# One-hot comparisons of a token sort on bfloat16 operands with the token tile as innermost index

## The chip, the cores and the metric

The kernel runs on one core of one Trainium2 chip. The metric is the device time of one execution in microseconds. Each kernel was executed several times; the median is what counts.

## The reference, cut to what matters

```python
x = L0_attn_x                      # (16, 256, 128) float32
xn = _layernorm(x)
s = attention(xn, ...)             # 16 heads of 8, LoRA weights, alibi slopes, causal, softmax
# routed feed-forward: each of the 4096 tokens belongs to one of 8 experts
indices = argmax(softmax(xn @ Wr + br))
for i in range(8):
    xi = xn * (indices == i)
    h = relu(xi @ W1[i] + b1[i])   # (128 -> 512)
    out += h @ W2[i] + b2[i]       # (512 -> 128)
return x + s * silu(out)
```

## The kernel before

The 4096 tokens are 32 tiles (`NT`) of 128 tokens; token tiles are sequences cut in two. The attention is a loop over `NB` = 16 sequences `i`, each with six groups `g` of score units; every engine's program is this same loop, and other work is hung into it by places `(i, g)` written out by hand at the top of the file. TensorE computes at the same time the scores of sequence i and the row maxima's scores of sequence i + 2. VectorE reduces those maxima (`unit_max`, L812). Four PSUM banks rotate for VectorE's results and three for ScalarE's, so TensorE waits for the reader of a bank's last use.

Beside this, the tokens are sorted by expert. `choose()` on VectorE (L925 to L929, place (1, 0)) makes the expert one-hot; `keep_logits` (L908, L913) comes just ahead of it. TensorE counts and ranks it (`count_tiles` L1213, `rank` L1220 and L1224), and VectorE works out for each token its slot: a tile of 128 rows (`SLOT_ROWS` = 40 of them) and a row in it (`token_slots`, L956 to L963). Then the inverse of this map is made with one-hot matrices:

- `tile_onehot` (VectorE, place (1, 4), L969 and L971) compares each token's slot tile with 0, 128, 256, ...; the second output is that one-hot times the token's place in its token tile.
- `tile_numbers` (GpSimd, place (1, 4), L546) multiplies the first in place by the token tile's number. `fill_v` (L540) and `max_parts` (L573 to L581) stand behind it in GpSimd's queue.
- `row_onehot(c)` (VectorE, L977, places (1, 5), (2, 0), (2, 1), (2, 2)) compares each token's row with 0 to 127, for eight token tiles at a time.
- `slot_tokens` (TensorE, place (2, 3), L1235) multiplies the two with 32 products, one for each token tile, which gives for each slot the token in it.
- `keep_ids` (VectorE, L983 to L988) turns that into `from_row` and `token_of`. GpSimd's `fetch_rows` (L532) gathers the rows by indirect DMA from (2, 4) on, TensorE turns them (`turn_rows`, L1351, first at (3, 2)) and the 39 expert tiles follow (`hidden` L1359, `output` L1367), one every few groups, almost to the end of the loop.

In the same places TensorE also projects sequence i + 4 (`project`, L1183), whose remainder VectorE takes (`remainder`, L856), ScalarE rounds (`second_part`, L658) and GpSimd splits once more (`third_part`, L519); and it makes the experts' constant rows at (2, 1) and (2, 2) (L1381, L1390). L511, L565 and L589 are GpSimd's memset and copies at the start, L522 its normalisation.

In the kernel before, the slot values are float32 (`r32`), the constants they are compared with are float32 for the tiles (`iota_slot`) and bfloat16 for the rows (`iota_row`), and the outputs are laid out with the token tile outside and the compared index innermost.

Of the kernel before, what the change touches and what calls it, by code (L numbers as in the profile page):

```python
# [25 lines left out]
BF16 = mybir.dt.bfloat16  # L26
I32 = mybir.dt.int32
U32 = mybir.dt.uint32
ALU = mybir.AluOpType
# [3 lines left out]
P = 128  # L33
NB, T, D = 16, 256, 128
NT = NB * T // P
# [6 lines left out]
E, HID = 8, 512  # L42
# [5 lines left out]
SLOT_ROWS = (SLOT_TILES + 3) // 4 * 4  # L48
# [4 lines left out]
ROUND = float(3 * P << 22)  # L53
# [64 lines left out]
CHOOSE_AT, COUNT_AT, RANK_AT, SLOTS_AT = (1, 0), (1, 1), (1, 2), (1, 3)  # L118
TILE_HOT_AT = (1, 4)
ROW_HOT_AT = {(1, 5): 0, (2, 0): 1, (2, 1): 2, (2, 2): 3}  # L120
IDS_AT, TILE_EXPERTS_AT = (2, 3), (2, 4)
PROJECT_FIRST = {6: 2, 8: 3}
TURN_FIRST = {(0, 4): 2, (0, 7): 3, (0, 9): 4}
# [86 lines left out]
def program(nc, x, w_dense, lora, br, b1, w_experts, const_f32, const_bf16, const_rows, zero_rows, out):  # L210
# [14 lines left out]
    with ctx:  # L225
        def sb(name, shape, dt=F32):
            return ctx.enter_context(nc.sbuf_tensor(name, shape, dt))

        def sem(name):
# [13 lines left out]
        iota_slot = cf[:, 2 * P + 8:2 * P + 8 + SLOT_ROWS]  # L243
        place1 = cf[:, 2 * P + 52:2 * P + 53]
        tile_ids = cf[:, 2 * P + 64:2 * P + 64 + NT]
# [9 lines left out]
        iota_row = cb[:, 2 * BLK + 2 * P + 2 * (NT + 1) * E + 2:]  # L255
# [7 lines left out]
        hT = sb("hT", [P, 2, NC_H, P])  # L263
# [25 lines left out]
        onehot_b = sb("onehot_b", [P, NT, E], BF16)  # L289
        tile_counts = sb("tile_counts", [P, 2, P], BF16)  # L290
        r32 = sb("r32", [P, 6, NT])
        r32i = sb("r32i", [P, 2, NT], I32)
        r40 = sb("r40", [P, 2, SLOT_ROWS])
        r8 = sb("r8", [P, 8, E])
        r8i = sb("r8i", [P, 2, E], I32)
        te_cmp = sb("te_cmp", [1, SLOT_TILES, E])
        te_f = sb("te_f", [1, 2, SLOT_TILES])
        tile_expert = sb("tile_expert", [1, SLOT_TILES], I32)
# [25 lines left out]
        xsT_slot = sb("xsT_slot", [P, 2, 4, P])  # L324
        crow_sb = sb("crow_sb", [P, D])
        w_flat = w_slots[:, :, :].rearrange("p r f -> p (r f)")
        row_hot = w_flat[:, 0:NT * P // 2].bitcast(BF16).rearrange("p (n m) -> p n m", m=P)
        tile_hot = w_flat[:, NT * P // 2:NT * P // 2 + NT * SLOT_ROWS].bitcast(BF16).rearrange("p (n c h) -> p n c h", c=2, h=SLOT_ROWS)
        rt = xs_slot[:, :, :, :].rearrange("p r j d -> p (r j d)")[:, 0:3 * NT * E].rearrange("p (c n) -> p c n", c=3)
        y_slot = sb("y_slot", [P, 3, D])  # L330
        y_tok = xn_all
# [3 lines left out]
        names = """x_in0 x_in1 x_in2 x_in3 x_in4 dense_in ident_in constants_in masks_in later_in br_in b1_in b1_pad b1_spread nmax_r2 zero_src lora_ps w_eff_done experts_in  # L335
            var_done std_done nmr_done dve_seq xn_vec xn_pool xn_act logits_turned_done part1_done part2_done part3_done
            q1_out0 q1_out1 q1_out2 q1_out3 q2_out0 q2_out1 q2_out2 q2_out3 q3_out0 q3_out1 q3_out2 q3_out3 nmax_zero max_zeroed0 max_zeroed1
            const_rows0 const_rows1 const_rows2 vd_zero vd_one onehot_done slots_done tile_place_done tile_hot_done row_hot_done rows_done tokens_done rows_kept tile_expert_done
            max_in0 max_in1 nmax1 nmax_r nmax2 nmax3
            v_done x_again0 x_again1 x_again2 x_again3 pv_ps pv_read rz_done o_norm_done oT_done b1_done b1_cols_done crow_diag_done  # L340
            w_done xs_in0 xs_in1 xs_in2 xs_in3 xs_in4 xs_in5 xs_in6 xs_in7 y_out0 y_out1 y_out2
# [2 lines left out]
        S = {n: sem(n) for n in names}  # L344
# [162 lines left out]
        def _(pool):  # L507
# [27 lines left out]
            def fill_v(b):  # L535
# [4 lines left out]
                pool.tensor_tensor(v_halves[b % 2][:, :, :, 0:DH], v_kept[:, b, :].rearrange("p (c d) -> p c d", d=DH).unsqueeze(2).to_broadcast(shape),  # L540
                                   of_half.unsqueeze(1).unsqueeze(3).to_broadcast(shape), ALU.mult).then_inc(S["v_done"], 1)

            def tile_numbers():

                pool.wait_ge(S["tile_place_done"], 1)
                pool.tensor_tensor(tile_hot[:, :, 1, :], tile_hot[:, :, 1, :], tile_ids.unsqueeze(2).to_broadcast([P, NT, SLOT_ROWS]),  # L546
                                   ALU.mult).then_inc(S["tile_hot_done"], 1)

            def scatter_y(t):
# [17 lines left out]
            def max_parts(b):  # L567

                r = b % 2
                for u in range(NU):  # L570
                    wait_vec_emptied(pool, "max", b, u)
                wait_act_full(pool, "nmax", b - 2)
                pool.tensor_scalar(nmax[r][:, :, 0, :], row_max[r][:, :, :], -1.0, None, ALU.mult).then_inc(S["nmax1"], 1)  # L573
                pool.wait_ge(S["nmax1"], b + 1)
                pool.tensor_tensor(nmax_rem[:, :, :], row_max[r][:, :, :], nmax[r][:, :, 0, :], ALU.add).then_inc(S["nmax_r"], 1)
                pool.wait_ge(S["nmax_r"], b + 1)
                pool.tensor_scalar(nmax[r][:, :, 1, :], nmax_rem[:, :, :], -1.0, None, ALU.mult).then_inc(S["nmax2"], 1)
                pool.wait_ge(S["nmax2"], b + 1)
                pool.tensor_tensor(nmax_rem2[:, :, :], nmax_rem[:, :, :], nmax[r][:, :, 1, :], ALU.add).then_inc(S["nmax_r2"], 1)
                pool.wait_ge(S["nmax_r2"], b - 1)  # L580
                pool.tensor_scalar(nmax[r][:, :, 2, :], nmax_rem2[:, :, :], -1.0, None, ALU.mult).then_inc(S["nmax3"], 1)  # L581
# [23 lines left out]
            for i in range(NB):  # L605
                for g, units in enumerate(GROUPS):
                    for t in FETCH_AT.get((i, g), ()):
                        wait_act_full(pool, "scores", i, units[0])
                        fetch_rows(t)
                    if g == PROJECT + 2 and i + AHEAD < NB:  # L610
                        third_part(i + AHEAD)
                    for t in range(SLOT_TILES):
                        if SCATTER_TURNS[t] == i * NG + g:
                            if g in (0, 3):
                                wait_act_full(pool, "scores", i, units[1])
                            elif TILES_AT[i, g][0] < SLOT_TILES:
                                wait_vec_full(pool, "hidden", TILES_AT[i, g][0])
                            scatter_y(t)
                    if g == 0 and 0 < i < NB - 1:
                        max_parts(i + 1)  # L620
                    if (i, g) == TILE_HOT_AT:
                        tile_numbers()
                    if i + 1 < NB and g == FILL_V:
                        fill_v(i + 1)
# [167 lines left out]
        def _(dve):  # L792
            seq = [0]

            def then(ins):

                seq[0] += 1
                ins.then_inc(S["dve_seq"], 1)
                dve.wait_ge(S["dve_seq"], seq[0])
# [65 lines left out]
            for n in range(2):  # L865
                last = dve.scalar_tensor_tensor(w_eff[:, n, :], pv_bank[:, n * P:(n + 1) * P], LORA_SCALE, w_raw[:, n, :], ALU.mult, ALU.add)
# [85 lines left out]
            def token_slots():  # L952

                maxima_between(*SLOTS_AT, 0)
                bank, emptied = wait_vec_full(dve, "rank")
                dve.tensor_tensor(m3[1], bank[:, 0:NT * E].rearrange("p (n e) -> p n e", e=E),  # L956
                                  r8[:, 4, :].unsqueeze(1).to_broadcast(shape), ALU.add).then_inc(emptied, 1)
                wait_vec_emptied(dve, "rank")
                then(dve.tensor_tensor(m3[2], m3[1], onehot_b[:, :, :], ALU.mult))
                chained(dve.tensor_reduce(r32[:, 3, :], m3[2], AX.X, ALU.add), SLOTS_AT, 1)  # L960
                then(dve.tensor_scalar(r32[:, 2, :], r32[:, 3, :], -(P - 1) / 2, ROUND, ALU.add, ALU.add))
                dve.scalar_tensor_tensor(r32[:, 5, :], r32[:, 2, :], ROUND, r32[:, 3, :], ALU.subtract, ALU.subtract)
                dve.tensor_scalar(r32[:, 4, :], r32[:, 2, :], ROUND, None, ALU.subtract).then_inc(S["slots_done"], 1)  # L963
                dve.wait_ge(S["slots_done"], 1)

            def tile_onehot():

                hot = [P, NT, SLOT_ROWS]
                then(dve.tensor_tensor(tile_hot[:, :, 1, :], iota_slot.unsqueeze(1).to_broadcast(hot),  # L969
                                       r32[:, 4, :].unsqueeze(2).to_broadcast(hot), ALU.is_equal))  # L970
                dve.tensor_scalar(tile_hot[:, :, 0, :], tile_hot[:, :, 1, :], place1, None, ALU.mult).then_inc(S["tile_place_done"], 1)  # L971

            def row_onehot(c):

                dve.wait_ge(S["later_in"], 16)
                hot = [P, 8, P]
                dve.tensor_tensor(row_hot[:, 8 * c:8 * (c + 1), :], iota_row.unsqueeze(1).to_broadcast(hot),  # L977
                                  r32[:, 5, 8 * c:8 * (c + 1)].unsqueeze(2).to_broadcast(hot), ALU.is_equal).then_inc(S["row_hot_done"], 1)

            def keep_ids():  # L980

# [17 lines left out]
            for b in range(2):  # L999
                for u in range(NU):  # L1000
                    if b == 0 or not STATISTICS_FIRST <= u < STATISTICS_FIRST + 3:
                        unit_max(b, u)
                    for n in MOMENTS_FIRST.get((b, u), ()):
                        last = moments(1 + n // 8, n, n + 1)
# [66 lines left out]
            for i in range(NB):  # L1071
                for g, units in enumerate(GROUPS):
# [44 lines left out]
                    if (i, g) in GATED_AT:  # L1117
                        c = GATED_AT[i, g]
# [11 lines left out]
            bank, _ = wait_act_full(dve, "s", NB - 1)  # L1130
# [6 lines left out]
        def _(pe):  # L1137
# [89 lines left out]
            def slot_tokens():  # L1227


                pe.wait_ge(S["tile_hot_done"], 1)  # L1230
                bank, full = begin_vec("ids")
                for n in range(NT):
                    if n % 8 == 0:
                        pe.wait_ge(S["row_hot_done"], n // 8 + 1)
                    last = pe.matmul(bank[:, 0:2 * SLOT_ROWS], row_hot[:, n, :], tile_hot[:, n].rearrange("p c h -> p (c h)"),  # L1235
                                     start=(n == 0), stop=(n == NT - 1))
                last.then_inc(full, 1)

# [315 lines left out]
```

## Time and profile before

| | |
|---|---|
| median of 3 runs | 296.31 us (295.81 to 296.85) |
| profiled execution | 296.07 us |
| its span, first to last instruction | 294.2 us |
| mean granted TensorE clock | 0.983 |
| TensorE busy | 267.8 us, 91% |
| VectorE busy | 228.1 us, 78% |
| ScalarE busy | 185.5 us, 63% |
| GpSimd busy | 152.6 us, 52% |

The span is shorter than the time, as the time also holds the start and the end of the program. Times of instructions are measured from the span's start. PE is TensorE, DVE VectorE, ACT ScalarE, POOL GpSimd.

### The profile page before, as it was taken

The page shows a single profiled execution, that of the slowest core. Times are in us where ns is not written, and L with a number is a line of the kernel's source. Part 1 is how long each engine was busy: PE and PEld are TensorE (multiplying, and loading weights), DVE is VectorE, ACT ScalarE, POOL GpSimd, SP SyncE. Part 2 cuts the span into 40 slices and gives each one's busy share as a digit, 9 for nine tenths or more (in the row PEclk, how much of TensorE's full clock was granted, in tenths as well). Part 3 has the DMA queues.
Part 4 walks back from the last instruction along what each step waited for, and adds up shares of the span by engine and source line. Part 5 has one row for each costly group of instructions (what it writes and reads, how often), then busy time and mean ns, then how long its engine had stood idle before and what let it go on. Part 6 is the DMA issues. An engine that isn't in the chain of part 4 may idle for free.

```text
span 294.2 us, 12787 instructions
## 1 busy us (share of the span) xinstructions
PE 267.8 (91%) x5196; PEld 203.6 (69%) x5196; DVE 228.1 (78%) x483; ACT 185.5 (63%) x331; POOL 152.6 (52%) x226
## 2 busy tenths in 40 slices
PE   7899999684996999999999999999999999979962
PEld 3556555353674788888887888888788888856641
DVE  3788999789987578596868768685875868676996
ACT  3335355444466668777777778777776876558960
POOL 3073293115436577866677667667766533343100
PEclk9999999979999799999999999999999999999997
DMA  4799556687415442332425433231524623108553
GB/s 137 207 240 212 127 166 194 203 240 225 112 36 134 109 126 67 95 97 57 108 55 129 123 101 84 74 91 51 133 51 96 147 54 90 30 29 250 138 163 111
DMA packets 50970, 35.98 MB, mean 122 GB/s; under 512 B 5112, under 2 KB 48376, under 8 KB 50784
## 3 DMA queue, kind: packets, MB, share of 16 engines
q1 hardware_dynamic: 46680, 28.89, 37.0%
q0 software_dynamic: 2496, 5.12, 7.0%
q10 hardware_dynamic: 1736, 1.15, 1.6%
q8 instruction: 42, 0.69, 1.0%
q14 instruction: 16, 0.13, 0.2%
HBM read 15.28 MB, written 6.75 MB: 75 GB/s over the span
## 4 chain that ended last, share of the span: by engine, by line
PE 68%; DVE 18%; issue 6%; DMA 3%; POOL 2%; SPq 1%; ACT 1%; ACTq 0%; DVEq 0%; POOLq 0%
PE bank L1359 14%; PE bank L1367 12%; PE bank L1273 11%; PE bank L1324 10%; PE bank L1183 4%; DVE row_max L812 4%; PE bank L1281 3%; PE bank L1343 3%; PE bank L1253 2%; PE bank L1190 2%; DVE xn_all L1063 2%; PE bank L1351 2%; DVE w_slots L977 2%; DVE xn_all L1057 1%; DVE o_turned L1020 1%
## 5 line engine op out<-in xcount | busy, mean ns | idle before, releaser
L812 DVE TENSOR_REDUCE row_max<-bank 128x2 f32<-128x512 f32 (+3 forms) x176 | 105.6, 627 | 19.2 <-PE bank L1261 16.3
L757 ACT ACTIVATE probs<-bank 128x512 f32<-128x512 f32 (+1 forms) x176 | 89.5, 558 | 46.4 <-PE bank L1281 46.1
L1273 PE MATMUL bank<-qk_stack 64*64 64x64 bf16 (+3 forms) x1024 | 60.8, 237 | 6.5 <-ACT probs L757 3.3
L1253 PE MATMUL bank<-qk_stack 64*64 64x64 bf16 (+3 forms) x1024 | 61.7, 237 | 1.1 <-DMA qk_stack<-parts 0.7
L554 POOL DMA_INDIRECT expert_rows<-y_slot,token_of x39 | 38.6, 990 | 37.2 <-PE bank L1359 22.8
L532 POOL DMA_INDIRECT xs_slot<-normalised_rows,from_row x39 | 39.7, 1018 | 24.9 <-PE bank L1281 17.9
L1273 PEld LDWEIGHTS bank<-qk_stack 64*64 64x64 bf16 x1024 | 34.3, 108 | 23.6 <-issue 10.7
L739 ACT ACTIVATE w_slots<-w_all 128x1156 f32 x39 | 45.5, 1167 | 4.0 <-issue 3.4
L1324 PE MATMUL bank<-probs,v_diag 128*32 128x64 f32 (+3 forms) x1024 | 46.5, 311 | 1.2 <-issue 1.0
L1045 DVE TENSOR_TENSOR hT<-bank,w_slots 128x512 f32<-128x512 f32 x39 | 27.0, 691 | 23.3 <-PE bank L1359 23.3
L1359 PE MATMUL bank<-xsT_slot,w_slots 128*128 128x128 f32 x312 | 44.6, 286 | 0.2 <-issue 0.2
L1281 PE MATMUL bank<-cb 64*64 64x128 bf16 (+2 forms) x352 | 43.7, 243 | 0.0
L1261 PE MATMUL bank<-cb 64*64 64x128 bf16 (+2 forms) x352 | 43.3, 243 | 0.0
L1367 PE MATMUL bank<-w_slots,hT 128*128 128x128 f32 x312 | 41.3, 276 | 0.0
L1359 PEld LDWEIGHTS bank<-xsT_slot,w_slots 128*128 128x128 f32 x312 | 38.0, 192 | 2.8 <-issue 0.8
L1367 PEld LDWEIGHTS bank<-w_slots,hT 128*128 128x128 f32 x312 | 38.0, 192 | 0.1
L1253 PEld LDWEIGHTS bank<-qk_stack 64*64 64x64 bf16 x1024 | 33.7, 108 | 5.6 <-issue 4.2
L1324 PEld LDWEIGHTS bank<-probs,v_diag 128*32 128x32 f32 x1024 | 25.2, 111 | 12.5 <-issue 2.3
L519 POOL TENSOR_TENSOR parts<-rem,parts 128x512 bf16<-128x512 f32 x15 | 17.5, 1165 | 18.0 <-ACT parts L658 17.7
L1183 PE MATMUL bank<-xnT_all,w_eff 128*128 128x256 f32 x64 | 17.8, 403 | 3.5 <-DVE row_max L812 2.7
L540 POOL TENSOR_TENSOR v_diag<-x_all,cf 128x512 f32<-128x512 f32 x16 | 17.9, 1118 | 6.0 <-ACT x_all L662 5.7
L1281 PEld LDWEIGHTS bank<-cb 64*64 64x64 bf16 x352 | 20.0, 109 | 0.0
(132 smaller groups left out, 346.1 us busy)
## 6 DMA issues: line engine op xcount, KB each, us to landing
qk_stack<-parts SPq DMA_DIRECT2D x120, 64.0 KB, 2.1
qk_stack<-parts SPq DMA_DIRECT2D x32, 128.0 KB, 2.8
w_all<-w_experts SPq DMA_DIRECT2D x8, 512.0 KB, 4.6
x_all<-x SPq DMA_DIRECT2D x7, 512.0 KB, 5.2
normalised_rows<-xn_all SPq DMA_DIRECT2D x4, 512.0 KB, 5.2
xn_all<-expert_rows SPq DMA_DIRECT2D x8, 256.0 KB, 5.2
out<-xn_all SPq DMA_DIRECT2D x7, 256.0 KB, 3.2
xs_slot<-normalised_rows,from_row POOLq DMA_INDIRECT x39, 3.2
```

Source lines behind the costliest of these rows:

```text
L532: pool.indirect_dma_start(xs_slot[:, q % 2, t % 4, :], None, xn_dram[:, :], bass.IndirectOffsetOnAxis(from_row[:, t:t + 1], axis=0)).then_ ...
L554: pool.indirect_dma_start(y_dram[:, :], bass.IndirectOffsetOnAxis(token_of[:, t:t + 1], axis=0), y_slot[:, t % 3, :], None).then_inc(S[f"y ...
L739: act.activation(w_slot[t % 3], w_all[:, bass.ds(e, 1), :].rearrange("p o f -> p (o f)"), ACT.Copy).then_inc(S["w_done"], 1)
L757: act.activation(probs[:, m % PROBS, 0:w], bank[:, 0:w], ACT.Exp).then_inc(emptied, 1)
L812: dve.tensor_reduce(row_max[b % 2][:, n, pairs[0]:pairs[-1] + 1], bank[:, 0:ln_u * len(pairs)].rearrange("p (c k) -> p c k", k=ln_u), AX.X ...
L1253: pe.matmul(bank[to, c * ln_u:(c + 1) * ln_u], q[rows, p, n * BLK:(n + 1) * BLK], k[rows, p, 0:(n + 1) * BLK], start=(c == 0), stop=False, ...
L1261: last = pe.matmul(bank[to, 0:ln_u * len(pairs)].rearrange("p (c k) -> p c k", k=ln_u)[:, :, n * BLK:], ident_b[rows, rows], mask_qk[rows] ...
L1273: pe.matmul(bank[rows, c * ln_u:(c + 1) * ln_u], k[rows, p, kb * BLK:(kb + 1) * BLK], q[rows, p, kb * BLK:], start=(c == 0), stop=False, s ...
L1281: last = pe.matmul(bank[rows, 0:ln_u * len(pairs)].rearrange("p (c k) -> p c k", k=ln_u)[:, :, 0:BLK], ident_b[rows, rows], mask_kq[rows]. ...
L1324: last = pe.matmul(pv_bank[32 * j:32 * j + 32, half * T + kb * BLK:(half + 1) * T], v_diag[b % 2][:, kb, p, :], probs[:, (b * NU + w) % PR ...
L1359: last = pe.matmul(bank[:, c * P:(c + 1) * P], w_slot[t % 3][:, c * P:(c + 1) * P], xsT_slot[:, t // 4 % 2, t % 4, :], start=(c == 0), sto ...
L1367: last = pe.matmul(bank[:, 0:D], hT[:, t % 2, c, :], w_slot[t % 3][:, W2 + c * D:W2 + (c + 1) * D], start=(c == 0), stop=(c == NC_H - 1))
```

## The change

The slot tile and the row of each token are written as bfloat16 into `place_slot`. Both one-hot arrays are laid out with the token tile innermost. The constants they are compared with, `iota_row` and `iota_slot`, are spread by GpSimd into full arrays, each number repeated 8 or 32 times, in bfloat16: 1024 and 1280 elements on each partition, at place (1, 1), in memory of `hT` and `xsT_slot` that isn't in use yet. VectorE then compares contiguous bfloat16 arrays with the slot values, repeated over the outer index. TensorE reads both operands of `slot_tokens` with a step: its weights every 8th element, its moving operand every 32nd. Two arrays that nothing uses are removed.

```diff
+IOTAS_AT = (1, 1)
...
-        r32i = sb("r32i", [P, 2, NT], I32)
+        place_slot = sb("place_slot", [P, 2, NT], BF16)
...
-        r8i = sb("r8i", [P, 2, E], I32)
...
-        row_hot = w_flat[:, 0:NT * P // 2].bitcast(BF16).rearrange("p (n m) -> p n m", m=P)
-        tile_hot = w_flat[:, NT * P // 2:NT * P // 2 + NT * SLOT_ROWS].bitcast(BF16).rearrange("p (n c h) -> p n c h", c=2, h=SLOT_ROWS)
+        row_hot = w_flat[:, 0:NT * P // 2].bitcast(BF16).rearrange("p (c m n) -> p c m n", m=P, n=8)
+        tile_hot = w_flat[:, NT * P // 2:NT * P // 2 + NT * SLOT_ROWS].bitcast(BF16).rearrange("p (c h n) -> p c h n", c=2, n=NT)
+        rows_iota = hT[:, 0].rearrange("p c k -> p (c k)").bitcast(BF16).rearrange("p (m n) -> p m n", n=8)
+        slots_iota = xsT_slot[:, :, :, :].rearrange("p r j k -> p (r j k)")[:, 0:SLOT_ROWS * NT // 2].bitcast(BF16).rearrange("p (h n) -> p h n", n=NT)
...
+            def spread_iotas():
+
+                pool.wait_ge(S["lora_ps"], 1)
+                pool.wait_ge(S["later_in"], 16)
+                pool.tensor_copy(rows_iota, iota_row.unsqueeze(2).to_broadcast([P, P, 8])).then_inc(S["iotas_done"], 1)
+                pool.tensor_copy(slots_iota, iota_slot.unsqueeze(2).to_broadcast([P, SLOT_ROWS, NT])).then_inc(S["iotas_done"], 1)
+
             def tile_numbers():
 
                 pool.wait_ge(S["tile_place_done"], 1)
-                pool.tensor_tensor(tile_hot[:, :, 1, :], tile_hot[:, :, 1, :], tile_ids.unsqueeze(2).to_broadcast([P, NT, SLOT_ROWS]),
+                pool.tensor_tensor(tile_hot[:, 1], tile_hot[:, 1], tile_ids.unsqueeze(1).to_broadcast([P, SLOT_ROWS, NT]),
                                    ALU.mult).then_inc(S["tile_hot_done"], 1)
...
-                dve.scalar_tensor_tensor(r32[:, 5, :], r32[:, 2, :], ROUND, r32[:, 3, :], ALU.subtract, ALU.subtract)
-                dve.tensor_scalar(r32[:, 4, :], r32[:, 2, :], ROUND, None, ALU.subtract).then_inc(S["slots_done"], 1)
+                dve.scalar_tensor_tensor(place_slot[:, 0, :], r32[:, 2, :], ROUND, r32[:, 3, :], ALU.subtract, ALU.subtract)
+                dve.tensor_scalar(place_slot[:, 1, :], r32[:, 2, :], ROUND, None, ALU.subtract).then_inc(S["slots_done"], 1)
...
-                hot = [P, NT, SLOT_ROWS]
-                then(dve.tensor_tensor(tile_hot[:, :, 1, :], iota_slot.unsqueeze(1).to_broadcast(hot),
-                                       r32[:, 4, :].unsqueeze(2).to_broadcast(hot), ALU.is_equal))
-                dve.tensor_scalar(tile_hot[:, :, 0, :], tile_hot[:, :, 1, :], place1, None, ALU.mult).then_inc(S["tile_place_done"], 1)
+                hot = [P, SLOT_ROWS, NT]
+                dve.wait_ge(S["iotas_done"], 2)
+                then(dve.tensor_tensor(tile_hot[:, 1], slots_iota, place_slot[:, 1, :].unsqueeze(1).to_broadcast(hot), ALU.is_equal))
+                dve.tensor_scalar(tile_hot[:, 0], tile_hot[:, 1], place1, None, ALU.mult).then_inc(S["tile_place_done"], 1)
...
-                dve.wait_ge(S["later_in"], 16)
-                hot = [P, 8, P]
-                dve.tensor_tensor(row_hot[:, 8 * c:8 * (c + 1), :], iota_row.unsqueeze(1).to_broadcast(hot),
-                                  r32[:, 5, 8 * c:8 * (c + 1)].unsqueeze(2).to_broadcast(hot), ALU.is_equal).then_inc(S["row_hot_done"], 1)
+                hot = [P, P, 8]
+                dve.tensor_tensor(row_hot[:, c], rows_iota, place_slot[:, 0, 8 * c:8 * (c + 1)].unsqueeze(1).to_broadcast(hot),
+                                  ALU.is_equal).then_inc(S["row_hot_done"], 1)
...
+                    if (i, g) == IOTAS_AT:
+                        spread_iotas()
...
-                    last = pe.matmul(bank[:, 0:2 * SLOT_ROWS], row_hot[:, n, :], tile_hot[:, n].rearrange("p c h -> p (c h)"),
+                    last = pe.matmul(bank[:, 0:2 * SLOT_ROWS].rearrange("p (c h) -> p c h", c=2), row_hot[:, n // 8, :, n % 8], tile_hot[:, :, :, n],
```

## Rows read from the trace of the kernel before

**Rows 1.** The profile's page, busy time of each engine in us, its share and instructions.
```profile
PE 267.8 (91%) x5196; PEld 203.6 (69%) x5196; DVE 228.1 (78%) x483; ACT 185.5 (63%) x331; POOL 152.6 (52%) x226
```

**Rows 2.** Stretch, length, busy us of PE, PEld, DVE, ACT, POOL; clock; DMA share.
```profile
60.00:61.50 1.50, 1.50 (x24) 0.77 (x16) 1.50 (x5) 0.86 (x2) 0.01 (x1) 0.50 0.91 180
...
70.80:73.40 2.60, 0.00 (x0) 0.00 (x0) 2.60 (x3) 0.83 (x2) 2.60 (x2) 1.00 0.46 108
...
83.80:95.70 11.90, 9.46 (x257) 6.49 (x257) 10.16 (x24) 8.10 (x16) 7.61 (x12) 1.00 0.36 92
...
97.00:260.00 163.00, 162.66 (x3180) 135.91 (x3183) 117.36 (x227) 117.68 (x192) 104.43 (x135) 0.99 0.34 87
```

**Rows 3.** Timeline of VectorE, 67 to 84 us: start, duration, instruction, idle time before it.
```profile
67.20 1.48 DVE L969 TENSOR_TENSOR w_slots<-cf,r 128x1280 bf16<-128x1280 f32 x1
68.72 0.55 DVE L971 TENSOR_SCALAR w_slots<-w_slots,cf 128x1280 bf16<-128x1280 bf16 x1
...
69.79 2.98 DVE L977 TENSOR_TENSOR w_slots<-cb,r 128x1024 bf16<-128x1024 bf16 x1
...
73.89 1.21 DVE L977 TENSOR_TENSOR w_slots<-cb,r 128x1024 bf16<-128x1024 bf16 x1
...
78.49 0.68 DVE L856 TENSOR_TENSOR rem<-bank,parts 128x512 f32<-128x512 f32 x1
...
80.36 1.86 DVE L977 TENSOR_TENSOR w_slots<-cb,r 128x1024 bf16<-128x1024 bf16 x1
...
83.86 0.20 DVE L983 COPY r<-bank 128x40 f32<-128x40 f32 x1 [0.65 <-PE bank L1235]
```

**Rows 4.** Timeline of TensorE, 73 to 95 us.
```profile
73.43 1.13 PE L1183 MATMUL bank<-xnT_all,w_eff 128*128 128x256 f32 x4 [2.71 <-DVE row_max L812]
...
79.32 2.02 PE L1390 MATMUL bank<-crow_sb,cf 128*128 128x128 f32 x16 [0.64 <-DVE rem L856]
...
82.50 1.32 PE L1235 MATMUL bank<-w_slots 128*128 128x80 bf16 x32
...
94.65 0.33 PE L1351 MATMUL bank<-cf,xs_slot 128*128 128x128 f32 x1 [1.73 <-DMA xs_slot<-normalised_rows,from_row]
```

**Rows 5.** Timeline of GpSimd, 53 to 86 us.
```profile
53.17 0.29 POOL L581 TENSOR_SCALAR nmax<-nmax_rem 128x32 bf16<-128x32 f32 x1
61.49 1.16 POOL L519 TENSOR_TENSOR parts<-rem,parts 128x512 bf16<-128x512 f32 x1 [8.04 <-ACT parts L658]
69.36 2.34 POOL L546 TENSOR_TENSOR w_slots<-w_slots,cf 128x1280 bf16<-128x1280 bf16 x1 [6.71 <-DVE w_slots L971]
...
79.99 1.16 POOL L519 TENSOR_TENSOR parts<-rem,parts 128x512 bf16<-128x512 f32 x1 [3.70 <-ACT parts L658]
85.37 1.18 POOL L532 DMA_INDIRECT xs_slot<-normalised_rows,from_row  x1 [4.23 <-issue]
```

**Rows 6.** Timelines of VectorE and TensorE around `choose()`.
```profile
55.24 0.22 DVE L913 TENSOR_TENSOR logits<-logits_turned,br_sb 128x64 f32<-128x64 f32 x1
...
55.95 0.42 DVE L926 TENSOR_TENSOR xs_slot<-logits,r 128x256 f32<-128x256 f32 x1
...
57.80 0.20 PE L1213 MATMUL bank<-cb,onehot_b 128*128 128x1 bf16 x2 [1.37 <-DVE onehot_b L929]
```

**Rows 7.** Timelines of VectorE and of GpSimd near 25 us.
```profile
25.13 0.93 DVE L913 TENSOR_TENSOR logits<-logits_turned,br_sb 128x64 f32<-128x64 f32 x1
...
24.83 1.15 POOL L519 TENSOR_TENSOR parts<-rem,parts 128x512 bf16<-128x512 f32 x1 [3.09 <-ACT parts L658]
```

**Rows 8.** Instructions of three lines on GpSimd, ns least/median/most.
```profile
L565 POOL COPY b_cols<-b_sb x4: 197/198/198, 31.0 to 31.4; 128x8 f32<-128x8 f32 x4
...
L589 POOL COPY v_diag<-cf x2: 288/288/289, 11.8 to 12.0; 128x64 f32<-128x64 f32 x2
...
L511 POOL MEMSET v_diag<- x2: 951/953/955, 0.9 to 1.8; 128x1024 f32 x2
```

**Rows 9.** The chain that ended last, in order of time: start, us, what.
```profile
106.44 1.09 PE bank L1359 x8
```

More of the change, by code:

```diff
@@ L337, in program @@
             q1_out0 q1_out1 q1_out2 q1_out3 q2_out0 q2_out1 q2_out2 q2_out3 q3_out0 q3_out1 q3_out2 q3_out3 nmax_zero max_zeroed0 max_zeroed1
-            const_rows0 const_rows1 const_rows2 vd_zero vd_one onehot_done slots_done tile_place_done tile_hot_done row_hot_done rows_done tokens_done rows_kept tile_expert_done
+            const_rows0 const_rows1 const_rows2 vd_zero vd_one onehot_done iotas_done slots_done tile_place_done tile_hot_done row_hot_done rows_done tokens_done rows_kept tile_expert_done
             max_in0 max_in1 nmax1 nmax_r nmax2 nmax3
```

## The prediction

> **What bounds the kernel now.** I read the busy shares first [rows 1]: TensorE is busy for 91% of the span, VectorE for 78%. That is an average, so I then read the stretches [rows 2]. From 97 to 260 us TensorE is busy for 162.66 of 163.00 us: nothing the diff touches runs there, and whatever moves the start of that stretch moves the end by as much. The edit sits ahead of it. From 70.80 to 73.40 us TensorE does nothing at all while VectorE is busy for all of it, and from 83.80 to 95.70 TensorE works 9.46 of 11.90 us.
>
> Next, the timeline of VectorE [rows 3]. From 67.20 until it waits for the products at 83.86 the listing marks no idle time, and both comparisons are in it: the tile comparison (1.48 us), its scaling (0.55), and four row comparisons of 1.21 us. Two of the four show more, 2.98 and 1.86. Beside them GpSimd runs L546 from 69.36 to 71.70 and L519 from 79.99 to 81.15 [rows 5]; 71.70 + 1.07 is 72.77, and 81.15 + 1.07 is 82.22, just where the two comparisons end. So a VectorE comparison with two SBUF inputs that starts while GpSimd reads SBUF waits for the whole GpSimd instruction.
>
> TensorE's timeline [rows 4] shows who waits for VectorE: projection L1183 at 73.43 after 2.71 us idle (its bank comes free from a maximum that stands behind the first row comparison), and L1390 at 79.32 after 0.64 us, released by L856, which stands behind the third. From 79.32 TensorE has no gap until the 32 products of `slot_tokens` at 82.50. These release L983 at 83.86, which leads to `from_row`; GpSimd starts its first fetch at 85.37 [rows 5], and fetches 0 to 3 with other work run one behind another until TensorE turns the rows at 94.65, after 1.73 us idle on that DMA. The chain that sets the end therefore goes: VectorE to 79.2, TensorE to 83.8, VectorE, GpSimd and DMA to 94.65, TensorE from there.
>
> **Removed: element time on VectorE.** L969 (1280 elements, 1.48 us) and L977 (1024, 1.21) give a line of 1.05 ns an element plus 0.14. After the change all operands are bfloat16 and innermost contiguous. The trace has no such two-input operation. Bounds: no gain, 1.21; or the rate of L971, 1280 bfloat16 elements with one input in 0.55, which is 0.32 ns an element and gives 0.47. Between them I take half the element time, as this one reads two streams where L971 reads one: 0.68 for a row comparison and 0.81 for the tile comparison, so 0.53 less for each of four and 0.67 less. The Trainium skill (VectorE: DVE Perf Modes, the perf-mode tier table) has `tensor_tensor` on bfloat16 in SBUF at twice the rate and never at four times, which is the value I take; no row here shows it. L971 itself, now on contiguous data, I leave at 0.55 (at most 0.07 to gain).
>
> What of this lies on the path: L969 ends 0.67 earlier, so L971, then GpSimd's L546, start 0.67 earlier (L546 keeps its 2.34). The first row comparison still waits for it and ends 0.67 + 0.53 = 1.20 earlier, at 71.57. L1183 goes with it, to 72.2. The second and third comparison add 1.07, so L856 ends 2.27 earlier, near 76.9. TensorE cannot follow all of that: after L1183, its work up to L1390 takes the same 5.25 us less the small wait of 0.06 for a maximum within it (none is then left), so L1390 comes at 77.3 to 77.4, 2.0 us earlier, now bound by TensorE. The fourth comparison is worth nothing: GpSimd's L519 comes after ScalarE's copy of L856's result, near 77.7 to 78.9, the comparison waits for it again and ends near 79.4, and `slot_tokens` comes at 80.5; what hides it is TensorE's own work from L1390 on, and without that cover 0.53 more would count. The fetches behind it are ordered by GpSimd and by TensorE's own scores, which shift alike. **Minus 2.0 us.**
>
> **Added: two copies on GpSimd.** `spread_iotas` stands at (1, 1), behind `max_parts(2)`, whose last instruction ends at 53.46 [rows 5]. Its semaphores are long set, so it starts near 53.5. GpSimd's next work is L519 at 61.49, so its own queue has room. The cost lies elsewhere: `choose()` runs on VectorE at that time, on the path, since TensorE waits 1.37 us for L929 before it can count [rows 6]. L913, L926, L927 and L929 have two SBUF inputs; L908, L925 and L928 have one or read PSUM. What that means is seen at 25.13: the same L913 takes 0.93 us instead of 0.22 and ends at 26.06, as L519 on GpSimd ends at 25.98 [rows 7]. The Trainium skill (SBUF — State Buffer, Who interferes with whom) says the same: a two-input VectorE instruction and a GpSimd one that reads SBUF exclude each other for the whole instruction. By that rule, too, nothing before 57.7 is safe unless the copies are done; the trace agrees.
>
> How long the copies take: GpSimd's COPY takes 198 ns for 8 elements and 288 for 64 [rows 8], which is 1.6 ns an element: 1.8 us for 1024, 2.2 us for 1280. The lower bound is a memset of 1024 in 0.95, which reads nothing: 0.95 and 1.2. At the COPY rate the first ends about 55.3, L913 (due at 55.24) slips in between, the second runs 55.5 to 57.7, and L926, due at 55.95, ends near 57.9 instead of 56.37: 1.5 us. If the second copy gets in ahead of L913, it is 57.5 against 55.46: 2.1 us. At the memset rate the second ends at 55.7 and L913 is held 0.4 us. I take **plus 1.5 us**, between 0.4 and 2.1, as the COPY rows are the same operation. It is passed on in full: VectorE, and TensorE behind L929, have no slack of that size before 66 us.
>
> **Changed: TensorE's operands in `slot_tokens`.** Weights now step 8 elements (16 bytes) and the moving operand 32 elements (64 bytes). Today 32 products with contiguous operands take 1.32 us, 41 ns each [rows 4]. No row has a strided operand. Bounds: nothing, and 136 ns each, the rate of a float32 product (8 in 1.09 us [rows 9]), which is 4.4 us, plus 3.0. The nearest row is the same product with contiguous data, so I stay near it, at half a doubling: **plus 0.65 us**. All of it is on the path. The Trainium skill (SBUF — State Buffer, Door 1: The DMA port swizzle) speaks against the change: it gives 16-byte cache lines and a penalty when each access goes to another line, as here in both operands. It names no factor; this is the third rival.
>
> **Sum.** -2.0 + 1.5 + 0.65 = +0.15 us on the profiled execution's 296.07 us (span 294.2 and 1.9 around it). The median of the runs shown is 296.31, so 0.24 above it; the sum gives 296.2 to 296.5 and I say 296.4. Removing `r32i` and `r8i` and the bfloat16 outputs of L962 and L963 (32 elements, fixed cost) change nothing. What a measurement can tell from no change is 0.3%, 0.9 us.
>
> **Cases.**
> 1. The saving is eaten by the copies and the strides: copies 1.5, strides 0 to 1.3. 295.5 to 297.3, likeliest 296.4; 0.42.
> 2. Faster: the copies run near the memset's rate and are over by 55.7. Then 0.4 replaces 1.5, and with unslowed products -2.0 + 0.4 = -1.6, 294.7. For it: every other GpSimd row has a second input, pointer scalars or scattered output, while these copies write in order. It decides from the point where the sum of copies and strides is under 1.1 us. 0.28.
> 3. The products slow down by a doubling or more. A doubling alone is 1.3 for 0.65, +0.8, 297.1; the float32 rate is 3.0, -2.0 + 1.5 + 3.0 = +2.5, 298.8. The row against it: weights of 128 columns load within 41 ns today, so there is spare rate. Slower from a total of 2.9 on: 0.14.
> 4. The second copy gets ahead of L913 (2.1) with a full doubling (1.3): +1.4, 297.7. TensorE's idle time before counting then also grows; its clock was granted at 0.50 (the 1.2 GHz level) from 60.00 to 61.50 [rows 2] after it had been mostly idle, so this may grow. 0.09.
> 5. The edit doesn't do what it says: the comparisons stay at one element a pass, the saving is nothing, +1.5 + 0.65 = +2.15, 298.5. For it: no two-input row is faster than 1.05 ns. Against: L971 shows that the engine does go faster on bfloat16. 0.07.
>
> Faster 0.28, same 0.42, slower 0.30. The range of 8 in 10, 294.6 to 298.2, takes in case 2 and leaves out the far parts of 3 and 5; the likeliest case's own is 295.5 to 297.3.
>
> **What the next profile would show.** Row comparisons of 0.68 us where GpSimd is quiet and the first ending with L546 (wrong: 1.21, or 0.47). Two COPY rows on GpSimd of 1.8 and 2.2 us from 53.5, and L913 or L926 lengthened by the wait, with `onehot_b` done near 59.2 instead of 57.7. L1390 no longer waiting for L856. The 32 products in 1.3 to 2.6 us. `slot_tokens` ending near 84. The prediction is wrong if VectorE isn't held during `choose()`, if the 32 products take over 4 us, or if TensorE at 97 us and later starts at a time not shifted by the sum of these.

## The result and the profile after

The changed kernel takes 298.69 us, median of 17 runs, against 296.31 us for the kernel before in as many: ratio 1.0077, 95% interval 1.0053 to 1.0101, so 1.6 to 3.0 us slower. This is outside the range of the prediction (294.6 to 298.2) and on the side to which it gave 0.30. The execution profiled took 297.37 us, the lowest of the 17, with a span of 295.5.

Most of the difference stands in the line of the 32 products of `slot_tokens`, in TensorE's timeline of the changed kernel (start, duration). Its lines are numbered anew: L1245 is what was L1235, L1193 was L1183, L1400 was L1390, L1361 was L1351, and L1334 was L1324, the products of the probabilities with the values.

```profile
72.71 1.13 PE L1193 MATMUL bank<-xnT_all,w_eff 128*128 128x256 f32 x4 [1.19 <-DVE row_max L823]
...
77.66 2.05 PE L1400 MATMUL bank<-crow_sb,cf 128*128 128x128 f32 x16
...
80.87 4.71 PE L1245 MATMUL bank<-w_slots 128*128 128x80 bf16 x32
...
86.73 1.51 PE L1334 MATMUL bank<-probs,v_diag 128*32 128x192 f32 x16
...
97.24 0.33 PE L1361 MATMUL bank<-cf,xs_slot 128*128 128x128 f32 x1 [1.45 <-DMA xs_slot<-normalised_rows,from_row]
```

Beside [rows 4]: the projection comes 0.72 us earlier, L1400 no longer waits and comes 1.66 us earlier, the products start 1.63 us earlier, at 80.87 for 82.50. Then they take 4.71 us instead of 1.32, 147 ns each instead of 41. What was 1.63 us early is 1.76 late. Behind them come the products with the values, L1334, which take 1.51 us (the same work took 0.86 before), in a stretch in which TensorE's clock was granted below its full 2.4 GHz level for part of the time: 0.72 of it on the mean from 84 to 88 us, where the kernel before had 1.00. This is the listing by stretch:

```profile
84.00:88.00 4.00, 4.00 (x68) 2.79 (x66) 2.28 (x9) 1.20 (x2) 0.88 (x1) 0.72 0.01 4
```

The last turn of fetched rows (L1361) comes at 97.24 for 94.65, 2.59 us late. So 0.83 us more are lost behind the products. The fetches show where: GpSimd's first starts 1.75 us late (87.12 for 85.37), its second 2.42 (90.22 for 87.80), with the low clock between them. In `after_again` below, where the clock stayed full there, the first and the second are both 2.8 us late.

VectorE's timeline shows the comparisons (L981 was L969, L987 was L977) and the hold ahead of `choose()` (L919 was L908, L924 was L913, L940 was L929). By a hold I mean that an instruction is lengthened because GpSimd reads memory at the same time:

```profile
53.95 0.45 DVE L919 STREAM_TRANSPOSE logits_turned<-bank 128x256 f32<-128x256 f32 x1 [0.84 <-PE bank L1212]
54.44 1.15 DVE L924 TENSOR_TENSOR logits<-logits_turned,br_sb 128x64 f32<-128x64 f32 x1
...
57.44 0.42 DVE L940 TENSOR_TENSOR onehot_b<-cf,r 128x256 bf16<-128x256 f32 x1
...
67.39 0.81 DVE L981 TENSOR_TENSOR w_slots<-xsT_slot,place_slot 128x1280 bf16<-128x1280 bf16 x1
...
69.31 2.75 DVE L987 TENSOR_TENSOR w_slots<-hT,place_slot 128x1024 bf16<-128x1024 bf16 x1
...
73.18 0.68 DVE L987 TENSOR_TENSOR w_slots<-hT,place_slot 128x1024 bf16<-128x1024 bf16 x1
...
78.57 1.33 DVE L987 TENSOR_TENSOR w_slots<-hT,place_slot 128x1024 bf16<-128x1024 bf16 x1
...
85.61 0.20 DVE L993 COPY r<-bank 128x40 f32<-128x40 f32 x1 [4.04 <-PE bank L1245]
```

Against [rows 3] the comparisons have the durations that were forecast, 0.81 and 0.68 us. The first still waits for GpSimd (2.75 us), and so does the last (1.33). The idle time in the last line is new: VectorE, which had been the engine in front, now sits idle for 4.04 us until the products are done. This is GpSimd's timeline (L549 and L550 are the two copies, L555 was L546, L534 was L532):

```profile
53.27 1.03 POOL L549 COPY hT<-cb 128x1024 bf16<-128x1024 bf16 x1
54.26 1.25 POOL L550 CAST xsT_slot<-cf 128x1280 bf16<-128x1280 f32 x1
...
68.87 2.63 POOL L555 TENSOR_TENSOR w_slots<-w_slots,cf 128x1280 bf16<-128x1280 bf16 x1 [6.10 <-DVE w_slots L982]
...
87.12 1.18 POOL L534 DMA_INDIRECT xs_slot<-normalised_rows,from_row  x1 [7.77 <-PE bank L1291]
```

The copies end at 55.51, and L924, due at 54.44, takes 1.15 us instead of 0.22 and ends at 55.59, 0.93 us late. L555 takes 0.29 us more than before [rows 5] in the new layout.

### The profile page after: what moved, and what is told of

Its sections match the earlier page's. It is cut to its first block, busy times and chain, and to the rows that moved or that the text cites. A ratio compares the mean times of both kernels' runs of the same rounds, so it can differ in the third digit from the quotient of the medians.

```text
span 295.5 us, 12790 instructions
## 1 busy us (share of the span) xinstructions
PE 272.2 (92%) x5196; PEld 207.3 (70%) x5196; DVE 226.6 (77%) x483; ACT 185.5 (63%) x331; POOL 154.2 (52%) x228
## 3 DMA queue, kind: packets, MB, share of 16 engines
q10 hardware_dynamic: 1736, 1.15, 1.6%
## 4 chain that ended last, share of the span: by engine, by line
PE 72%; DVE 16%; issue 4%; DMA 3%; POOL 1%; SPq 1%; ACT 1%; ACTq 0%; DVEq 0%; POOLq 0%
PE bank L1369 14%; PE bank L1377 12%; PE bank L1283 11%; PE bank L1334 11%; PE bank L1193 4%; DVE row_max L823 3%; PE bank L1291 3%; PE bank L1353 3%; PE bank L1263 2%; PE bank L1200 2%; DVE xn_all L1073 2%; PE bank L1361 2%; PE bank L1245 2%; DVE xn_all L1067 1%; PE bank L1167 1%
## 5 line engine op out<-in xcount | busy, mean ns | idle before, releaser
L534 POOL DMA_INDIRECT xs_slot<-normalised_rows,from_row x39 | 39.7, 1018 | 27.6 <-PE bank L1291 24.8
L1283 PEld LDWEIGHTS bank<-qk_stack 64*64 64x64 bf16 x1024 | 34.7, 109 | 23.8 <-issue 11.9
L1334 PE MATMUL bank<-probs,v_diag 128*32 128x64 f32 (+3 forms) x1024 | 46.8, 311 | 1.2 <-issue 1.0
L1369 PE MATMUL bank<-xsT_slot,w_slots 128*128 128x128 f32 x312 | 44.2, 285 | 0.2 <-issue 0.2
L1369 PEld LDWEIGHTS bank<-xsT_slot,w_slots 128*128 128x128 f32 x312 | 37.8, 191 | 2.8 <-issue 0.8
L1263 PEld LDWEIGHTS bank<-qk_stack 64*64 64x64 bf16 x1024 | 34.2, 108 | 5.5 <-issue 4.1
L1334 PEld LDWEIGHTS bank<-probs,v_diag 128*32 128x32 f32 x1024 | 25.1, 111 | 12.8 <-issue 2.6
L1291 PEld LDWEIGHTS bank<-cb 64*64 64x64 bf16 x352 | 20.1, 109 | 0.0
L1271 PEld LDWEIGHTS bank<-cb 64*64 64x64 bf16 x352 | 19.8, 109 | 0.0
```

The lines of the kernel that those rows point to most:

```text
L534: pool.indirect_dma_start(xs_slot[:, q % 2, t % 4, :], None, xn_dram[:, :], bass.IndirectOffsetOnAxis(from_row[:, t:t + 1], axis=0)).then_ ...
L1263: pe.matmul(bank[to, c * ln_u:(c + 1) * ln_u], q[rows, p, n * BLK:(n + 1) * BLK], k[rows, p, 0:(n + 1) * BLK], start=(c == 0), stop=False, ...
L1271: last = pe.matmul(bank[to, 0:ln_u * len(pairs)].rearrange("p (c k) -> p c k", k=ln_u)[:, :, n * BLK:], ident_b[rows, rows], mask_qk[rows] ...
L1283: pe.matmul(bank[rows, c * ln_u:(c + 1) * ln_u], k[rows, p, kb * BLK:(kb + 1) * BLK], q[rows, p, kb * BLK:], start=(c == 0), stop=False, s ...
L1291: last = pe.matmul(bank[rows, 0:ln_u * len(pairs)].rearrange("p (c k) -> p c k", k=ln_u)[:, :, 0:BLK], ident_b[rows, rows], mask_kq[rows]. ...
L1334: last = pe.matmul(pv_bank[32 * j:32 * j + 32, half * T + kb * BLK:(half + 1) * T], v_diag[b % 2][:, kb, p, :], probs[:, (b * NU + w) % PR ...
```

## The experiments

Twelve runs in three groups of four: nine other kernels, two of them measured twice, and the changed kernel once more. Each group was measured beside the kernel before on a chip of its own. The kernel before took 303.1 us in the first group, 296.1 in the second and 296.5 in the third, so ratios to it are compared, not times. Every listing has the line numbers of its own kernel. "Packed" below means that TensorE reads an operand's elements one next to the other.

**Which operand costs: `weights_packed` and `moving_packed`.**

```diff
-        row_hot = ....rearrange("p (c m n) -> p c m n", m=P, n=8)
+        row_hot = ....rearrange("p (n m) -> p n m", m=P)
...
-                dve.tensor_tensor(row_hot[:, c], rows_iota, place_slot[:, 0, 8 * c:8 * (c + 1)].unsqueeze(1).to_broadcast(hot),
+                dve.tensor_tensor(row_hot[:, 8 * c:8 * (c + 1), :], iota_row.unsqueeze(1).to_broadcast(hot),
+                                  place_slot[:, 0, 8 * c:8 * (c + 1)].unsqueeze(2).to_broadcast(hot), ...
```

> The changed kernel with the row one-hot back in its old layout (TensorE's weights contiguous) and its moving operand still stepping 64 bytes. Theory A, the moving operand's step is what costs: the 32 products stay near 4.7 us, and as the row comparisons are back at 1.21 us the kernel is some 3 to 4 us above the kernel before. Theory B, the weights' step is what costs: the products fall to some 1.3 us and the kernel is within 0.5 us of the kernel before. Theory C, both cost: 2 to 4 us.

`moving_packed` does the same to the tile one-hot and leaves the row one-hot as changed; its tile comparison then reads float32 constants again and takes 1.48 us.

> The changed kernel with the tile one-hot back in its old layout (moving operand contiguous) and the weights still stepping 16 bytes. Theory A (moving operand): products 1.3 us, kernel some 0.5 to 1 us below the kernel before, since the row comparisons stay at 0.68 us. Theory B (weights): products near 4.7 us, kernel 2 to 3 us above it. Theory C (both): 2 to 4 us of products.

`weights_packed`: ratio 1.0135 (1.0091 to 1.0178). `moving_packed`: 1.0017 (0.9982 to 1.0051). Their rows of the products in TensorE's timelines, first the one with contiguous weights:

```profile
82.19 4.54 PE L1245 MATMUL bank<-w_slots 128*128 128x80 bf16 x32
```

and then the one with a contiguous moving operand:

```profile
81.31 2.16 PE L1246 MATMUL bank<-w_slots 128*128 128x80 bf16 x32
```

So it is theory A for the size, with a part of C: the moving operand's step of 64 bytes alone makes 142 ns of each product, the weights' step of 16 bytes alone 68 ns, and both together are hardly more than the larger (147), not the sum. `moving_packed` was expected 0.5 to 1 us below the kernel before and is level with it within its interval: its weights cost 0.84 us and L924 is held for 0.93. In its profile the products end only 0.35 us before those of the kernel before (83.47 for 83.82).

`weights_packed` also has the row comparison on bfloat16 with one slot value repeated along the innermost index (a step of 0; ns least/median/most):

```profile
L987 DVE TENSOR_TENSOR w_slots<-cb,place_slot x4: 1209/1536/2498, 70.0 to 80.0; 128x1024 bf16<-128x1024 bf16 x4
```

Its least is 1209 ns, as with float32 slot values: the type alone buys nothing, the contiguous innermost index does.

**The copies alone: `copies_only`.** The kernel before with `spread_iotas` added and its semaphore waited for.

> The kernel before with the two GpSimd copies at (1, 1) and the wait for them added, and nothing else. If the hold of L913 is passed on in full, expert one-hot and all behind it come 0.9 us later and the kernel is 0.9 us above the kernel before. Rival: it is absorbed by TensorE's or the DMAs' waits up to 70 us, under 0.3 us.

Ratio 1.0013 (0.9985 to 1.0041). VectorE's timeline:

```profile
54.69 0.45 DVE L920 STREAM_TRANSPOSE logits_turned<-bank 128x256 f32<-128x256 f32 x1 [1.49 <-PE bank L1215]
55.18 0.49 DVE L925 TENSOR_TENSOR logits<-logits_turned,br_sb 128x64 f32<-128x64 f32 x1
```

The run doesn't tell the two readings apart by time (its interval holds 0 and 0.9 us), but the trace says why little is seen: here L925 came at 55.18, near the end of the copies, and was held 0.27 us. In the changed kernel's profile it came at 54.44 and was held 0.93. The 0.27 are passed on as far as the products, which start at 82.78 for 82.50.

**A layout between the two: `inner2`, `inner4`, `inner8`.** All comparisons stay contiguous in bfloat16, but only 2, 4 or 8 token tiles are innermost, in both one-hots. TensorE's steps become 4, 8 or 16 bytes, and the spread constants shrink with them (256 and 80 elements for two).

```diff
+IN = 2
...
+        row_hot = ....rearrange("p (c m n) -> p c m n", m=P, n=IN)
+        tile_hot = ....rearrange("p (c q h n) -> p c q h n", c=2, h=SLOT_ROWS, n=IN)
...
+                hot = [P, 8 // IN, P, IN]
+                dve.tensor_tensor(row_hot[:, 8 // IN * c:8 // IN * (c + 1)], rows_iota.unsqueeze(1).to_broadcast(hot),
+                                  place_slot[:, 0, 8 * c:8 * (c + 1)].rearrange("p (q n) -> p q n", n=IN).unsqueeze(2).to_broadcast(hot), ...
...
+                    ... row_hot[:, n // IN, :, n % IN], tile_hot[:, :, n // IN, :, n % IN], ...
```

> The changed kernel with only two token tiles innermost instead of 8 and 32: all operands of the comparisons still bfloat16 and contiguous innermost, TensorE's steps 4 bytes, the copied constants 256 and 80 elements. If the products pay for each access being on another 16-byte stretch, they fall back to 1.3 us; the copies end before L913's counterpart, so nothing is held in choose(); the comparisons keep 0.68 us, and the kernel is 1.5 to 2 us below the kernel before. Rival: any step but one element costs, products 3 us or more, kernel 1 us or more above it. Second rival: rows of two elements take the comparison back to 1.21 us, kernel as before.

> The kernel with two token tiles innermost once more, as a base for the three others: the interval of its ratio in the first run was 0.993 to 1.000. If the VectorE saving of some 2 us at the products is passed on, 0.993 to 0.997 of the kernel before; rival: given back by the granted clock, 0.999 to 1.002.

> Four token tiles innermost, both of TensorE's operands stepping 8 bytes, two of its elements in a 16-byte stretch. If what costs is an access in a new 16-byte stretch each time, the 32 products take 1.3 us as with a step of 4 bytes. Rival: the cost grows with the step, products between 1.4 and 2.4 us.

> Eight token tiles innermost in both, so the weights step 16 bytes as in the change and the moving operand 16 instead of 64. If the 16-byte stretch alone decides, the moving operand costs as much as at 64 bytes, 4.5 us for the products. Rival: the moving operand's cost depends on the size of its step, and at 16 bytes the products take what strided weights alone take, 2.2 us, or up to 3.

`inner2` gave 0.9963 (0.9926 to 1.0001) in the first group and 0.9946 (0.9911 to 0.9981) as `inner2_again`; `inner4` 0.9994 (0.9962 to 1.0026), `inner8` 1.0100 (1.0046 to 1.0155). The products of `inner2_again`, `inner4` and `inner8` in TensorE's timelines:

```profile
79.53 1.34 PE L1248 MATMUL bank<-w_slots 128*128 128x80 bf16 x32
```

```profile
81.22 2.60 PE L1248 MATMUL bank<-w_slots 128*128 128x80 bf16 x32
```

```profile
80.54 5.03 PE L1248 MATMUL bank<-w_slots 128*128 128x80 bf16 x32
```

This table has the 32 products by the step of the weights and of the moving operand, in bytes:

| weights | moving | kernel | us | ns each |
|---|---|---|---|---|
| 2 | 2 | before | 1.32 | 41 |
| 4 | 4 | inner2_again | 1.34 | 42 |
| 8 | 8 | inner4 | 2.60 | 81 |
| 16 | 16 | inner8 | 5.03 | 157 |
| 16 | 64 | after | 4.71 | 147 |
| 2 | 64 | weights_packed | 4.54 | 142 |
| 16 | 2 | moving_packed | 2.16 | 68 |

Where both operands step alike, 4 bytes are free, 8 double the product and 16 nearly double it again; taking the moving operand from 16 to 64 adds nothing. The clock is not the cause: it was granted in full during the products of the changed kernel, `after_again`, `strides_only` and `weights_packed`. Which operand makes the 81 ns at 8 bytes no run shows. For `inner4` my theory, that two elements in each 16-byte stretch are enough, was wrong, and its rival held in kind, though 2.60 us is above its 1.4 to 2.4. For `inner8` the theory held. The Trainium skill (SBUF — State Buffer, Door 1: The DMA port swizzle) has at least two accesses in a 16-byte line as enough to hide the memory's latency; here 8 bytes a step, two elements a line, costs 1.26 us over 32 products against 4 bytes, so the rows don't bear that part out, while they do bear out that 16 bytes and more are slow.

The comparison keeps its rate with rows of two elements, and with short copies L925 isn't held. The rows are those of `inner2`:

```profile
L989 DVE TENSOR_TENSOR w_slots<-hT,place_slot x4: 676/680/2448, 68.4 to 78.5; 128x1024 bf16<-128x1024 bf16 x4
L982 DVE TENSOR_TENSOR w_slots<-xsT_slot,place_slot x1: 815/815/815, 66.5 to 66.5; 128x1280 bf16<-128x1280 bf16 x1
...
54.67 0.23 DVE L925 TENSOR_TENSOR logits<-logits_turned,br_sb 128x64 f32<-128x64 f32 x1
```

**The products alone: `strides_only`.** The new layouts, but the comparisons read the constants unspread and there are no copies.

```diff
-                dve.tensor_tensor(row_hot[:, c], rows_iota, ...
+                dve.tensor_tensor(row_hot[:, c], iota_row.unsqueeze(2).to_broadcast(hot), ...
```

> The kernel before with nothing but the new layout of both one-hots: TensorE's operands step 16 and 64 bytes, while the comparisons read the constants unspread (innermost step 0) and no copies are made. If the products are what makes the change slower, they take 4.7 us here too, 3.4 us more on the path, and the kernel is 3 to 4 us above the kernel before (1.010 to 1.014), more than the changed kernel, which saves on VectorE. Rival: a part of the 3.4 us is absorbed by waits behind the products, under 1.006.

```profile
81.87 4.71 PE L1236 MATMUL bank<-w_slots 128*128 128x80 bf16 x32
```

**The changed kernel again, and with its copies on ScalarE: `after_again`, `copies_on_act`.**

> The changed kernel itself, as the control for the other runs of this call: 1.005 to 1.010 of the kernel before. Its profile also tells whether TensorE's clock falls right behind the slow products once more, as it did in the first profile (84 to 88 us at 0.72).

> The changed kernel with the two copies on ScalarE at (0, 5) instead of GpSimd at (1, 1). L913's counterpart takes 0.22 us again instead of 1.15. If that hold is passed on, the kernel is 0.9 us (0.3%) below the changed kernel of this call; rival: no difference, as the run with the copies alone had it (1.001 of the kernel before); second rival: slower, if ScalarE's 2 us of copies hold up its exponentials.

`strides_only` 1.0149 (1.0109 to 1.0189), `after_again` 1.0113 (1.0070 to 1.0157), `copies_on_act` 1.0074 (1.0045 to 1.0102). In `strides_only` the products take 4.71 us and the kernel is 3.2 to 5.6 us slower than before, a little above what was expected. That interval holds the 3.39 us of the products and excludes the rival, that a good part of them is absorbed behind them. Beside the products, GpSimd's product in place got slower by the layout (2.62 us for 2.34), and with it the row comparison that waits for it. `after_again` lies just above its expected 1.005 to 1.010, and the clock did not fall behind its products. `copies_on_act` is 0.4% below `after_again` by their ratios, but the intervals overlap, so that comparison is not decided. Its trace does show the hold gone:

```profile
54.62 0.23 DVE L925 TENSOR_TENSOR logits<-logits_turned,br_sb 128x64 f32<-128x64 f32 x1
```

and that of `after_again` shows it present, 0.88 us for the undisturbed 0.22:

```profile
55.73 0.88 DVE L924 TENSOR_TENSOR logits<-logits_turned,br_sb 128x64 f32<-128x64 f32 x1
```

**A version that beats both: `inner2_numbers`, and once more as `numbers_again`.** Two token tiles innermost, and the product with the tile number on VectorE, so that no GpSimd instruction stands in front of the first row comparison.

```diff
+                pool.tensor_copy(ids_b[:, :], tile_ids).then_inc(S["iotas_done"], 1)
...
+                dve.wait_ge(S["tile_place_done"], 1)
+                dve.tensor_tensor(tile_hot[:, 1], tile_hot[:, 1], ids_b[:, :].rearrange("p (q n) -> p q n", n=IN).unsqueeze(2).to_broadcast(hot), ALU.mult).then_inc(S["tile_hot_done"], 1)
...
-                        tile_numbers()
```

> Two token tiles innermost, and the product of the tile one-hot with the tile number moved from GpSimd to VectorE (bfloat16, 0.81 us), so that the first row comparison no longer waits for GpSimd. That comparison then takes 0.68 instead of 2.45 us, VectorE is 1 us further on, and if VectorE were the bound the kernel would be 1 us faster than with two innermost alone. Rival: the products come when TensorE has done its own work from the projection on, and the gain is what the projection comes earlier, 0.5 to 1 us; or nothing, if the clock or a DMA ends last.

> Two token tiles innermost and the tile numbers on VectorE once more, to settle whether it beats the kernel before and by how much: first interval 0.988 to 0.995, so 2 to 3 us below is expected; the rival is that a second call brings it to within 0.3%.

Ratios 0.9911 (0.9878 to 0.9945) and 0.9898 (0.9867 to 0.9930): 293.58 and 293.42 us, 1.6 to 3.6 and 2.1 to 3.9 us under the kernel before. These are VectorE's rows of `numbers_again`, by tile (ns least/median/most):

```profile
L985 DVE TENSOR_TENSOR w_slots<-hT,place_slot x4: 677/678/680, 69.8 to 77.3; 128x1024 bf16<-128x1024 bf16 x4
...
L980 DVE TENSOR_TENSOR w_slots<-w_slots,ids_b x1: 824/824/824, 68.5 to 68.5; 128x1280 bf16<-128x1280 bf16 x1
```

None of its four row comparisons waits any longer. Only for the first is that the edit's doing: in the profile of `inner2_numbers` the fourth is still held (1.33 us), as it meets GpSimd's part of the projection there. What the edit gains over `inner2` (ratios lower by 0.003 to 0.007, in different groups or with overlapping intervals) is likely but not shown.

## Why the prediction was wrong

The step that failed is a term of the sum, "half a doubling: plus 0.65 us" for the strided products. It measured **plus 3.39 us**. The mechanism was on the list as the third case, with a bound of 3.0 us taken from the float32 product, a chance of 0.14 and a time of 298.8, against 298.69 measured. That this time fits so well is partly luck: it has 0.39 us too little for the products and 0.57 too much for the copies. What failed was the choice within the bounds: "the nearest row is the same product with contiguous data, so I stay near it". That row shows nothing of a step. Even the far bound was too low, as 147 ns is more than the 136 of a float32 product. The row that I held against the case, that 128 weight columns load within 41 ns and so have rate to spare, says nothing of the moving operand, which costs most, and the weights' spare rate did not cover a step of 16 bytes either (68 ns).

The other steps, in the order of the prediction:

- **The comparisons run at twice the rate.** Right: 0.81 and 0.68 us for 1.48 and 1.21. The Trainium skill (VectorE: DVE Perf Modes, the perf-mode tier table) has this twofold rate, and the trace agrees. Case 5 is out.
- **The saving on the path, 2.0 us at L1390.** Nearly: 1.66 in the profile, where the expert one-hot was 0.12 late and L555 0.29 longer, which the first comparison waits for. Counted from the one-hot to the products, where the hold of L924 has no part, the saving is 1.75 us (57.44 to 80.87 for 57.32 to 82.50), and 1.73 in `after_again`. That it would be TensorE's own work which then bounds L1390, and that the fourth comparison would be worth nothing (1.33 us, held by GpSimd until before the products are due), were right. With nothing lost to slow products, in `inner2_again`, the kernel is 0.6 to 2.6 us faster.
- **The copies take 1.8 and 2.2 us.** Wrong: 1.03 and 1.25, near the memset's 0.95 and not at the rate of the small COPY rows. The case 2 mechanism was right, its result wasn't reached.
- **The copies hold `choose()` by 1.5 us.** Right in kind, and mis-sized: 0.93 us at L924 itself. The second copy did get ahead of L924, as in case 4, but costs 0.93 and not 2.1, as it is shorter. The traces show the hold passed on as far as the products: from the start of L919 to that of the products it is 26.92 us in the changed kernel and 26.67 in `after_again`, and 25.76 in `copies_on_act`, without a hold; the differences, 1.16 and 0.91, are even somewhat more than the holds of 0.93 and 0.66. How much of it reaches the end stays open: the copies alone cost under 0.41% and may cost nothing, and `copies_on_act` leaves it undecided. In the profile after, little is seen of it for another reason: VectorE's L919 starts at 53.95, and at 54.75 before, which makes up for most of the hold. In the other traces this start is between 53.9 and 55.3, with and without the change, so I don't take it for the change's doing; most of it is a wait of TensorE ahead of the router's products for which the profile shows no releaser (0.89 us in the kernel before, 0.23 in the changed one).
- **The sum.** The three measured terms, -1.75 for the saving, +0.93 for the hold and +3.39 for the products, give +2.57, and the medians are 2.38 apart. In the profiled pair the products end only 1.76 us late, as 0.80 of L919's earlier start comes on top. `strides_only` and `inner2_again` together, 4.4 and -1.6 us by their ratios, give 2.8, between the 2.3 of the first measurement and the 3.3 of `after_again`. These ratios have intervals of 0.7 to 1.3 us each way, so that the sums agree confirms none of the small terms.
- **TensorE from 97 us on is only shifted.** Not exactly. The rows are turned 2.59 us late in the profiled execution but its span is only 1.3 us longer. In the kernel before the clock was low from 96 to 98 and from 98 to 100 us, as these stretches show:

```profile
96.00:98.00 2.00, 2.00 (x40) 1.75 (x42) 1.12 (x2) 1.55 (x2) 1.71 (x2) 0.59 1.16 302
98.00:100.00 2.00, 2.00 (x37) 0.94 (x29) 1.33 (x2) 1.19 (x2) 1.76 (x2) 0.55 0.14 30
```

and in the changed one it was full from 96 to 100:

```profile
96.00:100.00 4.00, 2.59 (x73) 2.19 (x73) 2.22 (x5) 2.73 (x7) 2.61 (x3) 1.00 0.64 162
```

The second expert tile (`hidden`, L1359 before, L1369 after) shows that this is where the difference shrinks, from 2.59 to 1.04 us:

```profile
100.45 1.06 PE L1359 MATMUL bank<-xsT_slot,w_slots 128*128 128x128 f32 x8
```

```profile
101.49 1.06 PE L1369 MATMUL bank<-xsT_slot,w_slots 128*128 128x128 f32 x8
```

From there on the shift stays within 0.3 us of that. In `after_again` the clock was 0.72 from 96 to 100 us, the rows are turned 3.05 us late, and the span is 2.9 us longer. So a single profiled pair can be off by over 1 us from where the low clock falls, and only the medians carry the verdict.

## What to carry to other kernels

An index moved innermost for one engine becomes a step for another: before changing a layout for VectorE's bfloat16 rate, work out the byte step with which TensorE will read each operand. It isn't all or nothing: two elements innermost were enough for VectorE's 0.68 us, kept TensorE's step at 4 bytes and shrank the constants to be spread. And where the trace has no row like the operation added, the nearest row without the very property in question is not evidence for the low end.

## What the runs showed of the hardware that I had not expected

- The product of 80 columns pays for the byte step of its operands in grades: 41 to 42 ns up to 4 bytes, 81 at 8, 142 to 157 where the moving operand steps 16 or 64. The step of the weights alone costs less (68 ns at 16 bytes), and the two overlap.
- GpSimd's product in place, of 1280 elements, took 2.63 us in the layout with 32 token tiles innermost (2.64 with 8) and 2.34 in the old layout and with 2 or 4 innermost. I have no explanation for it.
- TensorE's clock was granted in full to the end of the slow products in the changed kernel (1.00 from 84.0 to 85.5 us), during which TensorE had no recorded gap, and at 0.55 from 85.5 to 88. The whole stretch from 84 to 88 had 0.72 there, 0.62 in `inner8`, 0.57 in `copies_on_act` and 0.86 in `strides_only` (0.71 from 88 to 92), but 1.00 in `after_again` and `weights_packed`, and 1.00 in the kernels with products under 3 us. That slow products bring the clock down is suggested by this, not shown.
